# Turning a low-rank weight with VectorE in place of TensorE, and gathering late weight blocks earlier, in a two-stage adapter kernel

## What is computed

```python
c = einsum('bsi,boi->bso', x, adapters[ids])
logits = c @ W_router.T                       # 8 experts, the best 2 by softmax, weights w
h = einsum('td,erd->ter', c, lora_A)          # rank 16
low = einsum('ter,eor,te->to', h, lora_B, w) * 2
x = x + c @ W_base.T + b_base + low
```

## Time and profile before

| | us |
|---|---|
| median of 3 runs | 610.05 (608.51 to 610.53) |
| the profiled execution | 609.52 |
| its span, first to last instruction | 607.5 |
| PE busy in the span | 592.5 (98%) |
| DVE busy | 471.5 (78%) |
| ACT busy | 145.1 (24%) |
| POOL busy | 127.1 (21%) |

### The profile page before, as it was taken

The page is one execution under the profiler, slowest core; times in us unless marked ns, Lnnn a source line. Parts: engine busy times, 40 slices in busy tenths (PEclk is TensorE's granted clock), DMA queues, the critical chain, the costliest instruction groups (busy, mean ns, idle before and its releaser), DMA issues.

```text
span 607.5 us, 13500 instructions
## 1 busy us (share of the span) xinstructions
PE 592.5 (98%) x4383; PEld 359.4 (59%) x4384; DVE 471.5 (78%) x1304; ACT 145.1 (24%) x291; POOL 127.1 (21%) x194
## 2 busy tenths in 40 slices
PE   4999999999999999999999999999999999999997
PEld 3444444444443444457776766767676767676773
DVE  3068779877987788698788897779987889887863
ACT  3000000200020002253232524235332235231324
POOL 4012222222110000070031222222221313131312
PEclk9999999999999999999999999999999999999999
DMA  7999998899899987020022232222222223221322
GB/s 256 411 407 324 315 307 310 327 323 303 313 407 408 357 307 244 21 79 23 14 74 89 68 94 62 92 70 89 71 86 69 88 66 96 67 89 62 94 71 87
DMA packets 43427, 106.90 MB, mean 176 GB/s; under 512 B 8450, under 2 KB 17666, under 8 KB 43394
## 3 DMA queue, kind: packets, MB, share of 16 engines
q1 hardware_dynamic: 31202, 76.57, 35.9%
q0 software_dynamic: 6784, 21.51, 10.8%
q10 hardware_dynamic: 5408, 8.43, 4.0%
HBM read 98.09 MB, written 8.39 MB: 175 GB/s over the span
## 4 chain that ended last, share of the span: by engine, by line
PE 91%; DMA 4%; DVE 3%; issue 1%; POOL 1%; DVEq 0%; SPq 0%
PE wide L544 30%; PE bank L651 20%; PE bank L659 10%; PE bank L739 8%; PE wide L722 8%; PE y_wide L575 4%; PE y_wide L697 3%; DMA ring<-adapters_dram 2%; PE wide L559 2%; DMA base_rows<-w_base_dram,perm_sb 1%; PE bank L672 1%; PE bank L675 1%; PE bank L671 1%; DVE c_pair L1107 1%; PE bank L752 1%
## 5 line engine op out<-in xcount | busy, mean ns | idle before, releaser
L544 PE MATMUL wide<-ring,x_in 128*64 128x512 f32 x960 | 209.6, 592 | 1.3 <-DMA ring<-adapters_dram 1.3
L544 PEld LDWEIGHTS wide<-ring,x_in 128*64 128x64 f32 x960 | 82.0, 137 | 117.2 <-issue 117.0
L1310 DVE STREAM_TRANSPOSE x_tok<-xres 32x128 f32<-32x128 f32 x464 | 140.2, 302 | 6.0
L1107 DVE STREAM_TRANSPOSE c_pair<-wide 32x256 f32<-32x256 f32 x240 | 107.0, 446 | 42.6 <-issue 20.4
L954 ACT ACTIVATE act_sb<-wide 128x512 f32<-128x512 f32 x120 | 66.5, 610 | 191.3 <-PE wide L722 191.3
L651 PE MATMUL bank<-c_hi,base_t 128*128 128x512 f32 x384 | 102.3, 390 | 0.0
L433 POOL DMA_INDIRECT xres<-xT_dram,row_in x32 | 35.0, 1095 | 230.8 <-DVE out_sb L1300 227.5
L651 PEld LDWEIGHTS bank<-c_hi,base_t 128*128 128x128 f32 x384 | 71.9, 188 | 15.3
L659 PE MATMUL bank<-c_lo,base_t 128*128 (+1 forms) x256 | 78.0, 390 | 0.0
L471 POOL COPY c_all<-c_pair 128x512 f32 x30 | 19.3, 669 | 211.2 <-DVE c_pair L1107 211.2
L868 ACT ACTIVATE small<-small 128x1 f32<-128x1 f32 x16 | 3.2, 202 | 214.5 <-DVE small L1143 214.5
(11 more groups left out here) (166 smaller groups left out, 604.1 us busy)
## 6 DMA issues: line engine op xcount, KB each, us to landing
ring<-adapters_dram SPq DMA_DIRECT2D x128, 512.0 KB, 5.8
x_in<-x_seq_dram ACTq DMA_DIRECT2D x30, 256.0 KB, 4.7
down_sb<-down_dram SPq DMA_DIRECT2D x32, 128.0 KB, 2.5
up_raw<-up_dram SPq DMA_DIRECT2D x62, 64.0 KB, 2.3
ar_sb<-lora_a_router_dram ACTq DMA_DIRECT2D x1, 544.0 KB, 4.4
x_in<-x_seq_dram SPq DMA_DIRECT2D x2, 256.0 KB, 5.6
mix_sb<-mix_dram SPq DMA_DIRECT2D x32, 16.0 KB, 2.0
xres<-xT_dram,row_in POOLq DMA_INDIRECT x32, 3.5
```

The costliest lines, as they stand in the source:

```text
L544: last = pe.matmul(acc[half][h][z * TOK:(z + 1) * TOK, :], x_in[:, half, z, k, :], ring[:, k, z, h * HALF:(h + 1) * HALF], start=(k == 0), ...
L1107: last = nc.vector.transpose(c_pair[r * SQ:(r + 1) * SQ, :, q * SQ:(q + 1) * SQ], wide[half][q * SQ:(q + 1) * SQ, :, :] .rearrange("p h (k ...
L1310: last = nc.vector.transpose(x1_tok[q * SQ:(q + 1) * SQ, :].rearrange("p (c f) -> p c f", f=P)[:, :, f * SQ:(f + 1) * SQ], xres[f * SQ:(f ...
```

## The change

Five things are edited. The low-rank B is turned by VectorE, with 16 transposes of 32x32 blocks in three pieces placed in pairs 12 to 14, into `b_lines` (the memory of `raw_tile`); ScalarE copies it back to `b_rows`, and `b_hi` and `b_lo` are made from there; TensorE's 8 transposes and their wait go. GpSimd gathers late base blocks 6 and 7 ahead of the copies of pairs 4 and 8 instead of behind them, and the last block of B in pair 10 instead of 8. The order of the base remainders is 0, 1, 4, 2, 3, with the fourth behind `out_of_acc` and the fifth behind `keep_last`; ScalarE starts `c_leading` after four and makes its last part after five; TensorE waits for four ahead of step 2. GpSimd's first gathers of `xres` wait for ScalarE's copy. `stay_busy` goes.

```diff
@@ -54,13 +54,13 @@
 BIG = -3.0e38
 SEQ_BITS = 5
 CS = KT // 2
-SPLIT_ORDER = (0, 1, 2, 4, 3, 5, 6, 7)
+SPLIT_ORDER = (0, 1, 4, 2, 3, 5, 6, 7)
 C_SLOT = 13
 SOON = 5
-BUSY = 8
 BATCHED = PAIRS - 4
 TILE_PIECES = (range(0, 6), range(6, 11), range(11, 16))
-GATHERS = {j + 1: (j,) for j in range(KT)}
+B_PIECES = (range(0, 4), range(4, 12), range(12, 16))
+GATHERS = {t: (j,) for j, t in enumerate((1, 2, 3, 4, 5, 6, 7, 10))}
 
 
 def build(nc, xT, x_seq, ids, adapters, w_base, b_base, lora_a_router, lora_b, mix, up, down, perm, out):
@@ -153,6 +153,7 @@
         b_lo = at(b_at, "b_lo", [P, KT, P], F32R)
         xres = at(region(8), "xres", [P, XBUF, GT])
         raw_tile = at(used[0] + start - 8192, "raw_tile", [P, D])
+        b_lines = at(used[0] + start - 8192, "b_lines", [P, KT, P])
         hw_lines = at(used[0] + start - 4096, "hw_lines", [P, 4, P])
         x1_tok_at = region(2)
         x1_tok = at(x1_tok_at, "x1_tok", [P, GT])
@@ -194,7 +195,6 @@
 
             return base_ps[j % 3]
 
-        b_ps = banks[0:2]
         sorted_ps = banks[0]
         u_ps, c_ps, d_ps = banks[0:4], banks[4], banks[7]
         y_ps = y_wide[:, :, 0:GT // 2].rearrange("f z (p t) -> f p z t", t=TOK)
@@ -218,8 +218,8 @@
         loads_ok, lists_ok, tile_in, tile_turned, hw_turned_ok, hw_placed = (
             sem(n) for n in ("loads_ok", "lists_ok", "tile_in", "tile_turned", "hw_turned_ok", "hw_placed"))
         rows_ok, row_in_step, row_out_step = (sem(n) for n in ("rows_ok", "row_in_step", "row_out_step"))
-        b_tr, b_hi_ok, b_ok, base_tr, base_turned, base_hi_ok, base_ok = (
-            sem(n) for n in ("b_tr", "b_hi_ok", "b_ok", "base_tr", "base_turned", "base_hi_ok", "base_ok"))
+        b_turned, b_placed, b_hi_ok, b_ok, base_tr, base_turned, base_hi_ok, base_ok = (
+            sem(n) for n in ("b_turned", "b_placed", "b_hi_ok", "b_ok", "base_tr", "base_turned", "base_hi_ok", "base_ok"))
         block_done, c_tok_ok, turn_done, c_pair_ok, c_kept, last_kept = (
             sem(n) for n in ("block_done", "c_tok_ok", "turn_done", "c_pair_ok", "c_kept", "last_kept"))
         router_done, gap_ok, tanh_ok, chain, hw_ok, hw_tr_done, hw_t_ok = (
@@ -461,6 +461,9 @@
 
             for j in range(SOON):
                 gather_base(j)
+            def gather_tile(i):
+                gather(raw_tile[:, :], w_base, perm_sb[:, i + SOON:i + SOON + 1], tile_in)
+
             def keep_pair(t):
 
                 seqs = [pool.value_load(order[0:1, 2, bass.ds(t + z * PAIRS, 1)], min_val=0, max_val=SEQS - 1)
@@ -473,17 +476,18 @@
 
             pool.wait_ge(order_ok, 1)
             for t in range(PAIRS - 1):
+                if t % 4 == 0 and 0 < t // 4 < KT - SOON:
+                    pool.wait_ge(tile_turned, t // 4)
+                    on_its_own()
+                    gather_tile(t // 4)
                 keep_pair(t)
-                if t % 4 == 0 and t // 4 < KT - SOON:
-                    j = t // 4 + SOON
-                    if t > 0:
-                        pool.wait_ge(tile_turned, t // 4)
-                    gather(raw_tile[:, :], w_base, perm_sb[:, j:j + 1], tile_in)
+                if t == 0:
+                    gather_tile(0)
                 for j in GATHERS.get(t, ()):
                     gather(b_rows[:, j, :], lora_b, perm_sb[:, j:j + 1], b_in)
                     gather(bias[:, j:j + 1], bias_rows, perm_sb[:, j:j + 1], bias_in)
             pool.wait_ge(rows_ok, 2)
-            pool.wait_ge(tile_turned, KT - SOON)
+            pool.wait_ge(b_placed, 1)
             pool.wait_ge(hw_placed, BATCHED * 2 + 8)
             for s in range(XBUF):
                 next_row(row_in, row_in_step, s, s)
@@ -591,11 +595,6 @@
                     pe.wait_ge(base_turned, j - 2)
                 transposes(base_set(j), [base_rows[:, j, k, :] for k in range(KT)], base_tr)
 
-            def stay_busy():
-
-                for _ in range(BUSY):
-                    pe.transpose(acc[0][1][:, 0:P], ident[:, :], ident[:, :])
-
             def pair(i, half):
 
                 t = i * 2 + half
@@ -613,7 +612,6 @@
 
             for j in range(SOON):
                 turn_base(j)
-            stay_busy()
             twin_blocks(range(KT))
             pe.wait_ge(loads_ok, 1)
             pe.wait_ge(base_turned, SOON)
@@ -634,8 +632,6 @@
             router(PAIRS - 2)
             adapter_blocks(PAIRS // 2 - 1, 1, range(5, 8), landed)
             turn_hw(PAIRS - 2)
-            pe.wait_ge(b_in, KT * 16)
-            transposes(b_ps, [b_rows[:, j, :] for j in range(KT)], b_tr)
             turn(PAIRS - 1)
             router(PAIRS - 1)
 
@@ -778,6 +774,7 @@
                 lora(0, 1)
                 pe.wait_ge(x1_ok, 1)
                 to_tokens(0, tr_ps)
+                pe.wait_ge(base_ok, 4)
                 base(0, 2, 0)
                 mix_tokens(0, 0)
                 base(0, 2, 1)
@@ -922,19 +919,18 @@
                     if n == 2:
                         tile_kept(i)
                         hw_put(i)
+            act.wait_ge(b_turned, 1)
+            nc.scalar.copy(b_rows[:, :, :], b_lines[:, :, :]).then_inc(b_placed, 1)
             for j in range(0, 5):
                 base_leading(j)
+            act.wait_ge(base_ok, 3)
+            act.wait_ge(b_placed, 1)
+            nc.scalar.copy(b_hi[:, :, :], b_rows[:, :, :]).then_inc(b_hi_ok, 1)
             tanh(PAIRS - 2)
             for j in range(5, 7):
                 base_leading(j)
             seqs = last_seqs(act)
             out_of_acc(PAIRS - 1, 1)
-            act.wait_ge(b_tr, 1)
-            act.wait_ge(base_ok, 4)
-            for h in range(2):
-                last = nc.scalar.copy(b_hi[:, h * KT // 2:(h + 1) * KT // 2, :],
-                                      b_ps[h][:, :].rearrange("p (j o) -> p j o", o=P))
-            last.then_inc(b_hi_ok, 1)
             turned(PAIRS - 1)
             keep_last(0, seqs)
 
@@ -979,11 +975,13 @@
             def step(g, j):
                 g1, j1 = (g, j - 1) if j >= 1 else (g - 1, STEPS - 1)
                 if early(g, j, 1):
-                    act.wait_ge(base_ok, 5)
+                    act.wait_ge(base_ok, 4)
                     act.wait_ge(c_kept, PAIRS * 2)
                     act.wait_ge(last_kept, 4)
-                    for part in range(CS):
+                    for part in range(CS - 1):
                         c_leading(g, part)
+                    act.wait_ge(base_ok, 5)
+                    c_leading(g, CS - 1)
                     tanh(PAIRS - 1)
                     base_leading(7)
                     up_leading(g, j)
@@ -1193,6 +1191,17 @@
                 if pieces[-1] == 15:
                     last.then_inc(tile_turned, 1)
 
+            def turn_b(pieces):
+
+                if pieces[0] == 0:
+                    dve.wait_ge(b_in, KT * 16)
+                for n in pieces:
+                    q, r = n // 4, n % 4
+                    last = nc.vector.transpose(b_lines[r * SQ:(r + 1) * SQ, :, q * SQ:(q + 1) * SQ],
+                                               b_rows[q * SQ:(q + 1) * SQ, :, r * SQ:(r + 1) * SQ])
+                if pieces[-1] == 15:
+                    last.then_inc(b_turned, 1)
+
             def turn_four(i, qs):
 
 
@@ -1224,25 +1233,27 @@
                     route(t, hw_four[:, (n + 1) % 4, :])
                     if n == 2:
                         turn_four(i, range(0, 1))
-            pair(PAIRS - 3, 1)
+            turn_b(B_PIECES[0])
+            turn_pair(PAIRS - 3, 1)
+            hw_turned(PAIRS - 4)
+            turn_b(B_PIECES[1])
+            route(PAIRS - 3)
+            turn_b(B_PIECES[2])
             turn_pair(PAIRS - 2, 0)
             for j in SPLIT_ORDER[0:3]:
                 base_rest(j)
             hw_turned(PAIRS - 3)
             route(PAIRS - 2)
-            base_rest(SPLIT_ORDER[3])
             seqs = last_seqs(dve)
             out_of_acc(PAIRS - 1, 1)
-            base_rest(SPLIT_ORDER[4])
+            base_rest(SPLIT_ORDER[3])
             turned(PAIRS - 1)
             keep_last(1, seqs)
+            base_rest(SPLIT_ORDER[4])
             hw_turned(PAIRS - 2)
             dve.wait_ge(b_hi_ok, 1)
-            for h in range(2):
-                ks = slice(h * KT // 2, (h + 1) * KT // 2)
-                last = nc.vector.tensor_tensor(b_lo[:, ks, :], b_ps[h][:, :].rearrange("p (j o) -> p j o", o=P),
-                                               b_hi[:, ks, :].bitcast(F32), ALU.subtract)
-            last.then_inc(b_ok, 1)
+            nc.vector.tensor_tensor(b_lo[:, :, :], b_rows[:, :, :], b_hi[:, :, :].bitcast(F32),
+                                    ALU.subtract).then_inc(b_ok, 1)
             dve.wait_ge(bias_in, KT * 16)
```

## The result

| | before | changed |
|---|---|---|
| median, 6 runs each | 609.47 us | 612.63 us (611.90 to 613.45) |
| ratio | | 1.0052, 95% interval 1.0042 to 1.0062 |
| profiled execution | 609.52 us | 611.90 us |
| its span; granted TensorE clock | 607.5 us; 1.000 | 609.9 us; 0.997 |

The changed kernel is slower by 3.2 us, 0.52%. The forecast, +0.65 us, lay inside "the same"; the measured difference is larger than the 0.3%, 1.8 us, that the forecast took as the least that can be told.

The account below looks back on a forecast made before the run. TensorE was taken to bound the kernel, 91% of the span. Start 0, early gathers -1.52 and change of stages +2.17 gave +0.65 us on the median of 610.05: 610.7 us, range 608.4 to 612.7.

Parts of the forecast that it names:

- Start, 0: Kernel start: dropping eight filler transposes gains 0, since the first adapter block's transfer releases the first adapter matmul.
- rival 3: Kernel start: without the filler TensorE starts the adapters at the lower clock, 2 us lost, 612.7 us; chance 0.05.
- Early gathers, -1.5: DMA-bound pairs around 180 us: moving the late gather earlier saves 1.52 us of queue time, so the adapter block lands sooner.
- The bounds of 0 and -1.78: Limits for the early gathers: 0 if something else delays the adapter block, -1.78 us if the wait goes altogether.
- VectorE's transposes, +2.3 at the last routing turn: Pairs 12 to 14: 16 transposes on VectorE make pair 14's turning and then TensorE's last routing turn 2.3 us late.
- What the change of stages gives back, net -0.1: Change of stages: c_tok gains 0.66 us, moved remainders cost 0.8, slack is 0.18; TensorE leaves it 2.2 us late.
- that sign of the forecast: Change of stages: weight loads of the c_lo matmuls would stall on VectorE.
- The port rule: Joined b_lo remainder: by the skill's exclusion with GpSimd the sum could be up to 1 us higher; taken at 0.
- The b_lo step: Joined b_lo remainder on VectorE, 1.22 against 1.28 us: bounds -0.1 to +0.3, taken at 0.
- Rival 1: Pairs around 180 us: adapter and x blocks replace the removed traffic, the 1.78 us wait remains, 612.3 us; chance 0.20.
- Rival 2: Pairs 12 to 14: VectorE's pieces are hidden, pair 14's turning is not late, 608.2 to 608.5 us; chance 0.17.

Follow-up runs that it names:

- experiment 1: Changed kernel with the 8 filler transposes of the start put back ahead of the first adapter matmuls: 613.51 us, ratio 1.0063.
- experiment 6: Changed kernel with 8 filler transposes at the change of stages and VectorE's last-pair register loads moved ahead of routing 14: 611.03 us, ratio 1.0025.
- experiment 2: Kernel before with only the early gathers: late base blocks ahead of the copies of pairs 4 and 8, B's last block in pair 10: 608.89 us.
- Experiments 9 and 10: Third late base block's gather cut from 512 to 64 KB: early-gather kernel 608.20 us; kernel before, at the old place, 608.70 us. Kernel before reprofiled: 609.79 us.
- Experiments 4 and 5: Changed kernel, no ScalarE copy of B: without VectorE's 16 transposes 608.95 us; with 12 of them and 8 TensorE filler transposes at the change of stages 609.59 us.
- experiment 3: Changed kernel with 8 identity transposes by TensorE behind the last routing turn, where the kernel before transposed B: 611.63 us, ratio 1.0030.
- experiment 4: Changed kernel without VectorE's 16 transposes of B and without ScalarE's copy back, B used unturned: 608.95 us, ratio 0.9986.
- experiment 7: Kernel before with early gathers, B on TensorE, the change's remainder order, register loads ahead of routing 14, b_lo after the c_lo parts: 608.79 us, ratio 0.9990.
- experiment 8: Kernel before with early gathers, new remainder order, b_lo after c_lo parts, last-pair register loads ahead of pair 14's turning, B on TensorE: 608.13 us, ratio 0.9975.

## Why the prediction was right or wrong, step by step

- **Start, 0.** The first adapter matmul waits for the ring in the changed kernel (16.66), and experiment 1 gains nothing. Right for the usual execution; rival 3 occurs, as the profile of experiment 6 shows, with 1.7 us of the 2 us priced. I had argued against it that dense matmuls follow at once; it fell as they began.
- **Early gathers, -1.5.** Right in sign, mis-sized: R gained 0.7 in the changed profile, the times 0.6 in experiment 2. The gather did start where I put it, its GpSimd instruction at 151.29. The failing step is "without 1.52 us of other traffic ahead of it, it lands at 185.3": it took 13.71 us to land instead of 14.43. I took queue time for arrival time. The queues stayed as full without it: from 160 to 180 us the adapter blocks' share rose from 87.0% to 94.1% and the x blocks' from 6.0% to 7.0%. Experiments 9 and 10 take most of the traffic away and gain about 1 us by the medians. The bounds of 0 and -1.78 held.
- **VectorE's transposes, +2.3 at the last routing turn.** Right to about 0.2 us. The pieces took 1.78, 3.58 and 1.79 us against 1.8, 3.6, 1.8; pair 14's turning was 2.47 us late; the wait at the router of pair 14 was 1.10 us against 1.2. The 0.80 us that I read ahead of hw_four stands in the row of the weight loads, where the changed kernel has 1.97; TensorE's matmuls wait 1.08 there, and did not wait before. Counted from pair 13's router, the last routing turn came 2.48 us late (268.30 - 242.89 against 267.17 - 244.24). Experiments 4 and 5 give 2.46 us for sixteen transposes and 1.95 for four of them.
- **What the change of stages gives back, net -0.1.** Wrong in one term. I let c_tok gain 0.66 us because no base remainder stood ahead of it. It gained 0.07: from TensorE's release by routing 14 to c_tok it was 268.16 - 267.17 = 0.99 us before and 269.22 - 268.30 = 0.92 after. The two register loads, which in the kernel before had lain beside the remainder (267.03 to 268.25), now stood bare for 0.97 us. I had allowed 0.47, from 0.34 of idle time at another place, where only part of two such loads was bare. Experiments 6 to 8 move them, and the gain appears in the last. S = 43.43 with the clock up is +2.8 instead of +2.2, and the missing 0.6 is this term. The rest of the step held with the clock up, the wait for `c_lo` included (experiment 3); in the changed kernel itself that sign of the forecast did not show, since the slow router covered it.
- **The clock, not in the sum: +0.9.** This is the term that was left out, and the largest of the three errors. I priced the clock only at the start and asked of TensorE's transposes of B only whether anything waited for them. They cost nothing, and they filled a wait that now came behind two longer ones. Experiment 3 shows the price, experiments 3 and 4 that both conditions are needed. It is the step that the eight transposes "ran while VectorE was copying c_tok": true, and half of what they did.
- **The port rule.** The b_lo step cost VectorE nothing: it took 1.21 us. The one who lost was GpSimd:

```profile
273.78 1.21 DVE L1255 TENSOR_TENSOR b_lo<-b_rows,b_hi 128x1024 fp32r<-128x1024 f32 x1
273.85 1.20 POOL L438 TENSOR_SCALAR row_in<-row_in 128x1 int32<-128x1 int32 x1 [0.19 <-POOL row_out L438]
```

 The same one-element GpSimd step took 0.21 us at 273.43 in the kernel before; here it ends when b_lo does. The Trainium skill ("SBUF — State Buffer", Summary: rules for kernel authors) has this as a full exclusion, in which the second to issue waits for the first to finish. The row agrees: b_lo began first, at 273.78, and kept its 1.21 us. GpSimd had time to spare.
- **Sum.** -0.7 against -1.5, +0.6 for the loads, +0.9 for the clock: 2.3 of the 2.5 us between the forecast's +0.65 and the measured +3.2. Two errors of size and one omission all pointed the same way. The time of 612.63 us still lies inside the range of 608.4 to 612.7, at its very edge, and that is luck: the upper end was drawn from rivals 1 and 3, a gather that gains nothing (it gained 0.6) and a clock fall at the start (it came at the change of stages), and the kernel before came out 0.6 us below the 610.05 from which the range was counted; the same difference counted from there would give 613.2, outside. Rival 1's mechanism, adapter and x blocks taking the place of the removed traffic, is what the DMA view shows; its price of the whole 1.5 us was about half right. Rival 2 was excluded as argued: pair 14's turning was 2.47 us late.

## What to carry to other kernels

An instruction that nobody waits for may still do something: filling a wait of TensorE is a use, and moving it to another engine both lengthens the waits and empties them. Count the lateness of the engine that feeds TensorE in its own chain; TensorE's cover at one place does not help if TensorE waits for that engine again further on. When an instruction is moved from ahead of a register load, look for what the load was hiding behind, and put the load where its engine idles before a semaphore, not behind one.

## What the runs showed of the hardware

The granted clock fell to 0.50 in the changed kernel with no single wait over 1.22 us: waits of 1.10, 1.08 and 1.22 us, with a router, adapter matmuls and two turns around them, came before the fall at about 271.2, while 1.23 and 0.79 us without the two others (experiment 4) did not lower it. Eight transposes of 1.09 us in all, in the third wait, made the difference (experiment 3). Two VectorE register loads took 0.97 us when nothing hid them, about 0.5 us each. The same two stood bare for 0.58 us together with two others behind a remainder that had waited for ScalarE (experiment 7), and for nothing ahead of pair 14's turning (experiment 8).
